# First attention: every second score bank gets its shift from a product with the identity on PE instead of an addition on DVE

## The reference

```python
q, k, v = (proj(xw, Wq, bq), proj(xw, Wk, bk), proj(xw, Wv, bv))
qn = q / jnp.maximum(jnp.linalg.norm(q, axis=-1, keepdims=True), 1e-12)
kn = k / jnp.maximum(jnp.linalg.norm(k, axis=-1, keepdims=True), 1e-12)
attn = jnp.einsum('whnd,whmd->whnm', qn, kn) * scale[None]
attn = attn + bias[idx].transpose(2, 0, 1)[None]
attn = attn.reshape(B, nh * nw, h, N, N) + mask[None, :, None]
attn = jax.nn.softmax(attn, axis=-1).reshape(B * nh * nw, h, N, N)
out = jnp.einsum('whnm,whmd->whnd', attn, v)
out = out @ Wo.T + bo
```

## Time and profile before

| what | us |
|---|---|
| median of 3 runs | 1012.9 (1008.73 to 1015.47) |
| the profiled execution's own time | 1015.97 |
| its span | 1014.0 |
| start of the first scores product | 72.6 |
| start of the last unit's scores | 200.64 |
| end of the last division | 212.1 |

### The profile page before, as it was taken

The page is one execution under the profiler, slowest core; times in us unless marked ns, Lnnn a source line. Parts: engine busy times, 40 slices in busy tenths (PEclk is TensorE's granted clock), DMA queues, the critical chain, the costliest instruction groups (busy, mean ns, idle before and its releaser), DMA issues.

```text
span 1014.0 us, 20687 instructions
## 1 busy us (share of the span) xinstructions
PE 855.2 (84%) x6419; PEld 478.1 (47%) x6440; DVE 830.1 (82%) x1720; ACT 697.0 (69%) x1318; POOL 604.0 (60%) x645
## 2 busy tenths in 40 slices
PE   4958888859999998788888987589999999999960
PEld 3433333424445763344355544255555556555640
DVE  7987888878866856687768888589999999999986
ACT  1867777736447556555777664288889999999966
POOL 1952222214787654277504777777777788888880
PEclk9978999979999999599999999599999999999985
DMA  6000000020003210000300000211111111111107
GB/s 246 1 2 2 2 2 2 2 79 0 1 1 114 70 44 0 1 2 1 100 1 14 27 26 26 61 56 47 39 45 41 33 34 35 33 35 36 36 21 250
DMA packets 25807, 39.64 MB, mean 39 GB/s; under 512 B 6436, under 2 KB 14632, under 8 KB 25448
## 3 DMA queue, kind: packets, MB, share of 16 engines
q1 hardware_dynamic: 16616, 28.93, 9.0%
q0 software_dynamic: 9088, 9.39, 2.8%
HBM read 24.83 MB, written 13.47 MB: 38 GB/s over the span
## 4 chain that ended last, share of the span: by engine, by line
PE 43%; DVE 23%; POOL 15%; issue 9%; ACT 7%; DMA 1%; POOLq 0%; SPq 0%; another core or an unknown queue 0%; ACTq 0%; DVEq 0%
PE bank L2495 9%; POOL results L808 6%; PE bank L2468 5%; POOL slots L785 4%; PE bank L2028 3%; DVE KSS L914 3%; POOL stage L767 3%; DVE stage L919 2%; PE bank L1945 2%; PE bank L1981 2%; DVE T L896 2%; PE bank L2045 1%; PE bank L2257 1%; PE bank L2070 1%; PE bank L1939 1%
## 5 line engine op out<-in xcount | busy, mean ns | idle before, releaser
L2495 PE MATMUL bank<-stage,big 128*128 128x512 f16 (+1 forms) x858 | 226.4, 384 | 6.9 <-issue 3.0
L808 POOL DMA_INDIRECT results<-T,small x156 | 177.7, 1139 | 44.3 <-issue 35.6
L785 POOL DMA_INDIRECT slots<-T,index x128 | 127.1, 993 | 79.3 <-DVE index L1347 41.4
L1855 ACT ACTIVATE T<-bank 128x512 f32<-128x512 f32 x234 | 139.5, 596 | 28.8 <-PE bank L2495 21.8
L1837 ACT ACTIVATE stage<-T 128x512 f16<-128x512 f32 x234 | 146.4, 626 | 3.5 <-DVE T L1494 2.1
L1494 DVE TENSOR_TENSOR T<-bank,T 128x512 f32<-128x512 f32 x195 | 133.8, 686 | 12.3 <-ACT T L1855 8.3
L1517 DVE TENSOR_TENSOR T<-T,stage 128x512 f16<-128x512 f32 x170 | 117.4, 690 | 1.2
L2495 PEld LDWEIGHTS bank<-stage,big 128*128 (+1 forms) x858 | 78.1, 101 | 59.1 <-issue 17.2
L692 POOL TENSOR_TENSOR stage<-T,small 128x512 f32<-128x512 f32 x32 | 34.2, 1068 | 99.0 <-PE bank L1945 99.0
L2468 PE MATMUL bank<-l2w,stage 128*128 (+1 forms) x936 | 90.8, 219 | 0.1
L2468 PEld LDWEIGHTS bank<-l2w,T 128*128 128x128 f16 x780 | 53.7, 98 | 69.3 <-issue 46.4
(11 more groups left out here) (395 smaller groups left out, 1970.9 us busy)
## 6 DMA issues: line engine op xcount, KB each, us to landing
stage<-slots SPq DMA_DIRECT2D x39, 130.0 KB, 2.1
stage<-in_w3l SPq DMA_DIRECT2D x8, 373.0 KB, 3.0
stage<-in_w1l SPq DMA_DIRECT2D x8, 320.0 KB, 3.0
results<-T,small POOLq DMA_INDIRECT x156
T<-in_xw SPq DMA_DIRECT2D x4, 512.0 KB, 6.1
X<-in_xi SPq DMA_DIRECT2D x1, 2048.0 KB, 13.4
slots<-T,index POOLq DMA_INDIRECT x128, 2.2
X<-results SPq DMA_DIRECT2D x8, 256.0 KB, 5.5
```

The source lines that it names most:

```text
L785: pool.indirect_dma_start(slots_d, bass.IndirectOffsetOnAxis(ap=index[:, k, n:n + 1], axis=0), rows5[:, n * RW:(n + 1) * RW], None).then_i ...
L808: pool.indirect_dma_start(results_d, bass.IndirectOffsetOnAxis(ap=IDS[t % 4][:, i:i + 1], axis=0), Y5[t % 2][:, i, :], None).then_inc(S(f" ...
L1855: nc.scalar.activation(S5[q][to], bank[q][r, :], ACT.Silu).then_inc(S("silu5"), 1)
L2495: mm = nc.tensor.matmul(to[0:m, :], big16[:, bass.ds(e * UPW + o, m)], XT[s], start=(v % 2 == 0), stop=(v % 2 == 1))
```

## The change

For every odd bank (the second of each unit) DVE no longer makes the addition. It computes the shift as before, now into a half-precision tile (`LV16`), and PE adds it to the score bank by a product of the identity with that tile, accumulated onto what is there (`lift`). ACT then takes the exp of the odd bank straight from PSUM. Even banks stay as they are, save that their result tile alternates by unit. `scores(u)` now waits until both banks of unit u-2 have gone through `exp_scores`, since the odd one is read there. The Ln and Exp of `invert_sums` now count on one semaphore instead of two.

```diff
-        LV = [spare[:, 1024 + 512 * s:1536 + 512 * s] for s in range(2)]
+        LV = spare[:, 1024:1536]
+        LV16 = spare[:, 1536:1792].bitcast(F16)
...
+            def level(b):
+                dve.wait_ge(*when("l0_summed", b + 1))
+                if b % 2 and b >= 3:
+                    dve.wait_ge(*when("l0_lifted", b // 2))
+                nc.vector.tensor_scalar(LV16 if b % 2 else LV, bank[4][:, :].bitcast(I32), LEVEL[0], LEVEL[1],
+                                        ALU.mult, ALU.add).then_inc(S("l0_level"), 1)
+
             def shift_down(b):
...
                 dve.wait_ge(*when("l0_level", b + 1))
-                if b >= 2:
-                    dve.wait_ge(*when("l0_exp", b - 1))
-                nc.vector.tensor_tensor(SC[b % 2], bank[2 * (u % 2) + g][:, :], LV[b % 2], ALU.add) \
+                if b >= 4:
+                    dve.wait_ge(*when("l0_exp", b - 3))
+                nc.vector.tensor_tensor(SC[b // 2 % 2], bank[b % 4][:, :], LV, ALU.add) \
                     .then_inc(S("l0_shifted"), 1)
...
                 if k <= UNITS:
+                    level(2 * k - 2)
                     shift_down(2 * k - 2)
...
                 if k <= UNITS:
-                    shift_down(2 * k - 1)
+                    level(2 * k - 1)
...
             def exp_scores(b):
                 u = b // 2
-                act.wait_ge(*when("l0_shifted", b + 1))
+                act.wait_ge(*when("l0_lifted" if b % 2 else "l0_shifted", u + 1))
                 if u >= 2:
                     act.wait_ge(*when("l0_pv", u - 1))
-                nc.scalar.activation(PX[b % 4], SC[b % 2], ACT.Exp).then_inc(S("l0_exp"), 1)
+                nc.scalar.activation(PX[b % 4], bank[b % 4][:, :] if b % 2 else SC[u % 2], ACT.Exp).then_inc(S("l0_exp"), 1)
...
             def scores(u):
                 pe.wait_ge(*when("l0_staged", u + 1))
                 if u >= 2:
-                    pe.wait_ge(*when("l0_shifted", 2 * (u - 1)))
+                    pe.wait_ge(*when("l0_exp", 2 * (u - 1)))
...
+            def lift(b):
+                pe.wait_ge(*when("l0_level", b + 1))
+                nc.tensor.matmul(bank[b % 4][:, :], ident16[:, 0:128], LV16,
+                                 start=False, stop=True, skip_group_check=True).then_inc(S("l0_lifted"), 1)
...
                     weigh(k - 2)
+                if 1 <= k <= UNITS:
+                    lift(2 * k - 1)
```

More of the change, by code:

```diff
@@ L909, in _ @@
             runs = [(0, 0, SS, WS), (1, 0, SS + WS, WS - SS), (1, WS - SS, 0, SS)]
+            def level(b):
[4 more added lines that the diff above has]
+                                        ALU.mult, ALU.add).then_inc(S("l0_level"), 1)
             def shift_down(b):
[L912 to L915, removed]
                 dve.wait_ge(*when("l0_level", b + 1))
-                if b >= 2:
-                    dve.wait_ge(*when("l0_exp", b - 1))
-                nc.vector.tensor_tensor(SC[b % 2], bank[2 * (u % 2) + g][:, :], LV[b % 2], ALU.add) \
+                if b >= 4:
+                    dve.wait_ge(*when("l0_exp", b - 3))
+                nc.vector.tensor_tensor(SC[b // 2 % 2], bank[b % 4][:, :], LV, ALU.add) \
                     .then_inc(S("l0_shifted"), 1)
             def divide_unit(u):
-                dve.wait_ge(*when("l0_rsum", u + 1))
+                dve.wait_ge(*when("l0_rsum", 2 * u + 2))
                 nc.vector.tensor_tensor(T34[:, 256 * u:256 * u + 256], bank[5 + u % 2][:, 0:256], RS[u % 2],
@@ L1589, in invert_sums @@
                     act.wait_ge(*when("l0_out", u - 1))
-                nc.scalar.activation(RS[u % 2], bank[5 + u % 2][:, 256:512], ACT.Ln).then_inc(S("l0_lnsum"), 1)
-                act.wait_ge(*when("l0_lnsum", u + 1))
+                nc.scalar.activation(RS[u % 2], bank[5 + u % 2][:, 256:512], ACT.Ln).then_inc(S("l0_rsum"), 1)
+                act.wait_ge(*when("l0_rsum", 2 * u + 1))
                 nc.scalar.activation(RS[u % 2], RS[u % 2], ACT.Exp, scale=-1.0).then_inc(S("l0_rsum"), 1)
```

## The result

| | before | changed |
|---|---|---|
| median, us (10 runs each) | 1014.85 (1008.73 to 1016.78) | 1018.08 (1016.44 to 1023.1) |
| ratio | | 1.0048, 95% interval 1.0025 to 1.0070 |
| profiled execution, us (span) | 1015.97 (1014.0) | 1017.13 (1015.2) |

The changed kernel is about half a percent slower. It was forecast as slower by less than 1%, and 1018.1 us lies in the range of 1015 to 1028. The medians differ by 3.2 us and the means by 4.8 (by the interval, 2.5 to 7.1), against +7.6 predicted. Where they come from is read from the traces: the start of the first, the fourth and the last unit's scores, and the end of the last projection. "3 turns" is the first to the fourth scores, "28 turns" the fourth to the last, "end" the last scores to the end of the last projection.

The account below looks back on a forecast made before the run. The loop was taken as bound by a ring of waits ending with DVE's addition ahead of the scores, no engine being full. Turns +6.9, start +1.7, end -1.0 gave +7.6 us on 1012.9: 1020.5 us, range 1015 to 1028.

Parts of the forecast that it names:

- The new ring: Loop: odd bank's level, new product behind the weighing, exp, next scores; a plain turn of 4.02 us.
- the larger bound, from DVE: Hand-over from ACT to PE in the loop: 0.15 as after DVE, against 0.05 in the nearest row; 0.08 taken.
- The product on PE: New identity product in the loop: starts at +2.88 directly behind the weighing and takes 0.39 us.
- The projection turn: Loop turns with a projection: 5.17 us where they took 4.91, the product adding a slot of 0.25.
- DVE's relief at nothing: Loop: DVE's 22 us of removed additions are worth nothing beyond the path they lay on; 1.1 us of room.
- The start, +1.7: First turns at the half clock: 0.6 us longer up to the next scores, then 1.1 in the following turn.
- The end, -1.0: Behind the last scores: shorter PE pauses may keep the full clock, 0 to -3.3 us; -1.0 taken.
- the bound of -3.3: Largest gain allowed at the loop's end if the last weighing and projection run at the full clock.
- even: Loop's end: one DVE addition less gives 0.6 us, but the last exp waits for a product (0.14 + 0.39 + 0.07).
- The difference goes through in full: Behind the loop: what follows hangs on the loop's end, so the whole +7.6 us reaches the total.
- the rival: The clock drops in the loop: two half-clock turns give 1026 us, all 28 give 1096; chance 0.07.

Follow-up runs that it names:

- e4: The changed kernel plus an unused 128x512 addition on DVE behind the odd bank's level in each unit; ratio 1.0058 to the kernel before.
- e5: The kernel before with unused 128x512 products filling PE's three pauses behind the last scores; ratio 0.9970 to the kernel before.
- e2: The kernel before with one wait changed: scores wait for the exp of both banks two units back; ratio 1.0096 to the kernel before.
- e3: The changed kernel with the identity product serving the even bank and DVE's addition the odd one; 1005.81 us, ratio 0.9924 to the kernel before.
- e7: The changed kernel with the new product ahead of the weighing instead of behind it; ratio 1.0177 to the kernel before.

## Why the prediction was right, and where its sizes were off

- **The new ring: right.** The scores' wait for the exp was named as what would set the turns, with 4.02 us for a plain one; 4.04 was measured. Two hand-overs were off and made up for each other in part: PE answers ACT after 0.14 (131.01 + 0.60 to 131.75) instead of 0.08, and ACT answers PE after 0.03 (130.59 + 0.39 to 131.01) instead of 0.07. I had the row for ACT to PE from an idle PE at the half clock; the larger bound, from DVE, was nearer.
- **The product on PE: right.** 0.39 long, at +2.88, directly behind the weighing.
- **The projection turn: 0.13 too long.** 5.04 against 5.17: the slot is 0.22 (134.63 to 134.85) and the projection, with the half-sum, then takes 1.94 to the next scores and not 2.04. Seven times 0.13 is 0.9 us, twenty-one times 0.02 is 0.4 the other way; together the 28 turns came out 0.5 below the forecast.
- **DVE's relief at nothing: right in the turns**, shown by e4; at the end of the loop it is worth more than the working gave it. The sum of rows gave 1.1 us of room, and an addition of 0.69 fits.
- **The start, +1.7: not to be seen.** The first three turns vary between traces of one kernel by 1.3 and 1.8 us, as much as the term.
- **The end, -1.0: the term that was mis-sized.** It measured -3.35 to -3.45 (11.64 and 11.63 against 14.99 and 15.08). The working put the clock at 0.92 for the weighing and 1.47 for the projection, 2.4 together; the bound of -3.3 that it gives is more than these rows add up to, so its nearness to -3.35 is luck. It took -1.0 "since the pause ahead of the projection stays". That pause stayed (1.41 us in both), and the clock held through it: it had fallen before the last weighing, not in that pause. e4 brought it down again, e5 kept it up in the kernel before by filling. The other part, the way to the last weighing, was put at "even" and measured -1.03: the working added the product to that way and did not take off the addition, which the product replaces.
- **"The difference goes through in full": wrong for the projection.** The 3.35 us are 1.4 to 2.0 at the next layer's product.
- **The sum.** 6.44 less 1.4 to 2.0 is 4.4 to 5.0 us, with the start left out. The means differ by 4.8 and the medians by 3.2, and the interval of 2.5 to 7.1 takes in both. That 6.44 - 3.35 comes to 3.1, near the 3.2 of the medians, is no proof.

On the clock within the loop the rival fell: 1.00 in all traces between 100 and 190 us, with a pause of 0.56 in every plain turn of the changed kernel and 0.94 in e2's, against the swings that the Trainium skill tells of ("TensorE: Matmul & The Clock Gate", "A second HAM failure mode: psum-queue depth-cycling"). At the end of the loop e5, and e4 in one trace, show that PE's pauses move the clock; the same page's section "Part 1: The HAM clock gate" says that the gate is set by how busy PE has recently been, and e5's trace, where nothing but the filling changed, agrees.

Left open: what in these pauses decides. The clock held with idle stretches of 1.04, 0.18 and 0.69 us (changed kernel, two traces) and with 1.76 and 0.95 (e3), and fell with 1.64 and 0.18 (e4) and with 0.88 and 1.19 (e7). Neither the longest stretch nor their sum puts these in order, so e4 and e3, one trace each, do not show that 0.6 us more of idleness is the cause.

## What to carry to other kernels

Before moving work from one engine to another, write down the ring that ends the wait, step by step with start times from one turn, and see who reads the buffer last in the new form: here the freed addition was 0.69 us, and the exp that took its place as the last reader cost more. Of two equal buffers relieve the one whose consumer has slack; the same edit on the even bank took 2.7 us off the 28 turns where on the odd one it added 6.4. And at the edge of a loop look at the clock of PE's last products, and follow a gain there into the next layer before counting it: of 3.35 us only 1.4 to 2.0 got there.

## What of the hardware was not expected

- ACT's exp of 128x512 takes 0.597 us from PSUM and 0.621 from SBUF (medians of 32 each in the changed kernel).
- Instructions of one engine that don't depend on each other start closer than they last: ACT's half exp, 0.60 long, is followed by the next after 0.49 (129.39 to 129.88), so in this loop a sum of durations overstates ACT's part of a ring by 0.1 for each.
- The hand-overs differ by direction: 0.03 from PE to ACT, 0.14 from ACT to PE, 0.15 from DVE to PE. They are not constant within one: 0.07 from PE to ACT in the earlier trace rows behind the scores, 0.05 from ACT to PE in the earlier trace rows.
- A DVE operation of 128x16 took 1.00 us beside POOL's cast of 128x1152 from 32 to 16 bits, and 0.17 without it (L321 and L320 behind the loop).
